# Causal mask of a self attention: TensorE's mask matmuls replaced by VectorE's add-and-maximum, head by head

## The reference, cut to what matters

```python
causal_bias = jnp.where(i[None, :] <= i[:, None], 0.0, NEG)[None, None]
for l in range(N_LAYERS):
    h = rmsnorm(x, n1[l])
    qkv = h @ Wqkv[l].T + bqkv[l]
    q, k, v = jnp.split(qkv, 3, axis=-1)
    q = apply_rope(split_heads(q, H), cos, sin)
    k = apply_rope(split_heads(k, H), cos, sin)
    s = jnp.einsum('bhqd,bhkd->bhqk', q, k) * scale + causal_bias
    o = merge_heads(softmax(s) @ split_heads(v, H)) @ Wo[l].T + bo[l]
    x = x + o
    # ... cross attention with 77 keys, then a gated feed forward
```

## Time and profile before

| | |
|---|---|
| median of three runs | 2097.03 us (2095.99 to 2102.07) |
| the profiled execution's own time | 2108.02 us |
| its span | 2106.3 us |
| mean granted TensorE clock | 0.936 of full speed |
| busy: TensorE / VectorE / ScalarE / GpSimd | 86% / 67% / 51% / 37% |
| self attention of layers 0, 1, 2, 3 begins (first reduction of maxima) | 657, 1029, 1366, 1699 us |

### The profile page before, as it was taken

The page is one execution under the profiler, slowest core; times in us unless marked ns, Lnnn a source line. Parts: engine busy times, 40 slices in busy tenths (PEclk is TensorE's granted clock), DMA queues, the critical chain, the costliest instruction groups (busy, mean ns, idle before and its releaser), DMA issues. The chain is left out here.

```text
span 2106.3 us, 34605 instructions
## 1 busy us (share of the span) xinstructions
PE 1821.6 (86%) x12966; PEld 1123.3 (53%) x12971; DVE 1414.7 (67%) x3427; ACT 1067.3 (51%) x1523; POOL 785.3 (37%) x1131
## 2 busy tenths in 40 slices
PE   5978998584787898899899899999989999989978
PEld 4556665363454444565544464644555554456557
DVE  8667676552776877875577874577786466787475
ACT  2655655121453465564466566366656446656510
POOL 4423334403613554431455341255443154533130
PEclk9999998587787899999999999999999999999989
DMA  7443343121000000132000033000014000004200
GB/s 226 112 135 101 103 108 94 52 77 43 23 1 13 1 1 13 32 101 56 16 1 1 1 95 81 28 1 2 1 53 117 7 16 2 1 24 101 52 1 21
DMA packets 69995, 100.91 MB, mean 48 GB/s; under 512 B 17126, under 2 KB 35438, under 8 KB 69188
## 3 DMA queue, kind: packets, MB, share of 16 engines
q1 hardware_dynamic: 60612, 90.01, 14.9%
q0 software_dynamic: 9216, 8.69, 1.6%
HBM read 52.43 MB, written 12.38 MB: 31 GB/s over the span
## 5 line engine op out<-in xcount | busy, mean ns | idle before, releaser
L1778 DVE TENSOR_REDUCE maxima<-wide 128x2 f32<-128x512 f32 (+3 forms) x512 | 405.9, 818 | 133.7 <-PE wide L831 130.3
L2014 ACT ACTIVATE prob<-wide 128x768 f32<-128x768 f32 (+1 forms) x384 | 332.1, 881 | 146.0 <-PE wide L831 145.9
L1937 ACT ACTIVATE prob<-wide 77x1024 f32<-77x1024 f32 x256 | 257.8, 1017 | 91.9 <-PE wide L831 87.5
L831 PE MATMUL wide<-q_g 32*128 32x256 f32 (+3 forms) x2048 | 266.1, 390 | 38.2 <-ACT prob L2014 18.1
L2256 POOL TENSOR_SCALAR_AFFINE_SELECT prob<-prob 128x256 f32<-128x256 f32 (+1 forms) x384 | 184.8, 487 | 292.6 <-ACT prob L2014 291.0
L1454 DVE TENSOR_REDUCE maxima<-wide 128x8 f32<-128x616 f32 x256 | 202.8, 795 | 115.0 <-PE wide L831 109.4
L831 PEld LDWEIGHTS wide<-q_g 32*128 32x128 f32 x2048 | 138.4, 186 | 203.7 <-issue 99.8
L2078 POOL TENSOR_TENSOR rstd<-moments,cst 128x4 f32<-128x4 f32 x88 | 90.4, 1027 | 364.2 <-DVE moments L1342 171.5
L1858 ACT ACTIVATE q_g<-wide 128x1024 fp32r<-128x1024 f32 x128 | 131.1, 1024 | 185.0 <-PE wide L831 185.0
L831 PE MATMUL wide<-kx,q_g 128*128 128x312 f32 x512 | 180.7, 418 | 8.3 <-DVE maxima L1454 5.8
L2163 POOL DMA_DIRECT2D masked_k<-kx x224 | 121.3, 546 | 178.2 <-PE wide L831 177.0
(11 more groups left out here) (249 smaller groups left out, 3087.2 us busy)
## 6 DMA issues: line engine op xcount, KB each, us to landing
masked_q<-q_g SPq DMA_DIRECT2D x448, 64.0 KB
masked_q<-mask_l SPq DMA_DIRECT2D x84, 308.0 KB
masked_k<-kx POOLq DMA_DIRECT2D x224, 19.5 KB, 1.9
A<-in_w SPq DMA_DIRECT2D x2, 2048.0 KB, 11.9
unit_w<-in_unit_w SPq DMA_DIRECT2D x8, 448.0 KB, 3.8
ffn_w<-in_ffn_w SPq DMA_DIRECT2D x4, 768.0 KB, 4.7
slots_in<-v_third SPq DMA_DIRECT2D x1, 2560.0 KB, 12.4
prob<-slots_in SPq DMA_DIRECT2D x8, 320.0 KB, 3.3
```

The lines of the kernel that those rows point to most:

```text
L831: return e.matmul(out, lhsT, rhs, start=start, stop=stop, is_transpose=turn)
L1778: e.tensor_reduce(top[:, t, h], v[:, :, at0:at0 + P * t + P], AX.X, ALU.max, negate=True).then_inc(*made("max", *([("free", tile)] if t == ...
L1937: e.activation(p[0:SC, :], s[0:SC, :], ACT.Exp, bias=0.0, scale=1.0).then_inc(*made("exp", pb, ("free", tile)))
L2014: e.activation(pv, sv, ACT.Exp, bias=0.0, scale=8 ** -0.5).then_inc(*made("exp", pb, ("free", tile)))
```

## The change

TensorE's mask matmuls are gone, and with them the bf16 mask `causal_b` and its cast at the start. The constant "causal" is twice as wide: 512 bf16 numbers packed in 256 words, zeros for 384 keys and then the triangle, so that its last n columns are the mask of a block of n keys. VectorE reads the scores of one head and one block from PSUM, adds that mask, writes the sum back to the same place in PSUM and gives the maximum of the row: `tensor_tensor_reduce`, 16 in a group in place of 8. It has no negation, so that the maxima are stored as they are and the rows of the keys hold -1 in place of 1.

```diff
-for _n, _w in (("ident", P), ("causal", P), ("cumul", P), ("cos", NI * 8), ("sin", NI * 8),
+for _n, _w in (("ident", P), ("causal", S // 2), ("cumul", P), ("cos", NI * 8), ("sin", NI * 8),
...
+        causal = const("causal").bitcast(BF)
...
-                        mm(s[:, at1:at1 + P * t + P], qk[r, 0, P * t:P * t + P], qk[r, 1, 0:P * t + P],
-                           start=t == blocks[0], stop=False)
+                        i_mm = mm(s[:, at1:at1 + P * t + P], qk[r, 0, P * t:P * t + P], qk[r, 1, 0:P * t + P],
+                                  start=t == blocks[0], stop=t == blocks[-1])
                     at0 += P * t + P
-
-                for c in range(2):
-                    bank = s[:, S * c:S * c + S].rearrange("p (i k) -> p i k", i=NI)
-                    i_mm = mm(bank[:, blocks[0]:blocks[0] + len(blocks), :], ident_b[:, :],
-                              causal_b[:, :].unsqueeze(1).broadcast_to([P, len(blocks), P]), start=False)
                 i_mm.then_inc(*made("scores", tile))
...
-            e.tensor_copy(causal_b[:, :], const("causal")).then_inc(*made("begin"))
...
                 for t in blocks:
-                    e.tensor_reduce(top[:, t, h], v[:, :, at0:at0 + P * t + P], AX.X, ALU.max, negate=True).then_inc(
-                        *made("max", *([("free", tile)] if t == blocks[-1] else [])))
-                    at0 += P * t + P
+                    n = P * t + P
+                    for c, i in enumerate(heads_in):
+                        part = s[:, S * c + at0:S * c + at0 + n]
+                        e.tensor_tensor_reduce(part, part, causal[:, S - n:S], 1.0, NEG, ALU.add, ALU.max,
+                                               top[:, t, i:i + 1]).then_inc(
+                            *made("max", *([("free", tile)] if (t, c) == (blocks[-1], 1) else [])))
+                    at0 += n
...
-                e.memset(k_tok[:, :, :, MROW:MROW + 2], 1.0).then_inc(*made("clear"))
+                e.memset(k_tok[:, :, :, MROW:MROW + 2], -1.0).then_inc(*made("clear"))
...
-    put("causal", np.where(r[None, :] > r[:, None], NEG, 0.0))
+    late = np.concatenate([np.zeros((P, S - P)), np.where(r[None, :] > r[:, None], NEG, 0.0)], 1).astype(np.float32)
+    put("causal", (late.view(np.uint32) >> 16).astype(np.uint16).view(np.float32))
```

More of the change, by code:

```diff
@@ L156 @@
     tensor_reduce = tensor_copy = memset = reciprocal = bn_stats = bn_aggr = affine_select = dma_start = anything
-    indirect_dma_start = anything
+    indirect_dma_start = tensor_tensor_reduce = anything
 def interleaved(items):
@@ L532, in build @@
         ident_b = sb("ident_b", [P, P], BF)
-        causal_b = sb("causal_b", [P, P], BF)
         cumul_b = sb("cumul_b", [P, 2 * P], BF)
@@ L1772, in causal_max @@
                 heads_in, blocks = CAUSAL_TILES[k]
-                h, at0 = slice(heads_in[0], heads_in[-1] + 1), 0
-                v = s[:, :].rearrange("p (i k) -> p i k", i=2)
+                at0 = 0
                 for w in need(tile):
```

## The result

The changed kernel takes 2147.39 us (median of four runs, 2144.1 to 2151.03). Four runs of the kernel before on the same chip have a median of 2099.55 (2095.99 to 2104.32). The ratio is 1.0227, 95% interval 1.0196 to 1.0258: 48 us slower. The forecast was slower, 2125 us with 2072 to 2235 as its range.

The account below looks back on a forecast made before the run. TensorE was taken to bound the steady groups before, changing places with VectorE after. Terms of +10, +9 and +10 us gave +29, rounded to +28: 2097 + 28 = 2125 us, range 2072 to 2235.

Parts of the forecast that it names:

- TensorE's saving: Six pairs of mask matmuls gone from each head group: about 1.4 us a group, 5.6 us a batch less TensorE time.
- The pair's fixed part: Fixed cost of each new two-instruction VectorE operation, 16 a group: taken as 0.16 us, between 0.14 and 0.31.
- The lower end: Lowest cost thought possible for a new VectorE pair, both instructions overlapping with neighbours: 0.07 + 0.07 = 0.14 us.
- The built-in waits of the ring: VectorE waits in the ring of three tiles: 0.4 us before tile three, 0.66 before tile five, together 1.1 a group.
- The steady batch: Four successive head groups go from 45.74 to 46.5 us, 0.8 more; 12 such batches give +10 us.
- The first batch: First batch of layers 1 to 3: 2.0 us for the VectorE-filled group, about 1 for the rest; 3 x 3 = +9.
- Layer 0: Its first five groups, where VectorE is the bound already, pay 2.0 us each: +10 us.
- The clock: Side term: a mean TensorE clock of 0.9 adds some 4 us to its batch, which VectorE's 41 still cover.
- A: Rival: TensorE's time wins, a pair costs 0.14 us, the wait before tile three vanishes; faster, 2080 us; chance 0.24.
- B: Rival: VectorE's pairs don't overlap, 0.31 us each; much slower, 2265 us, or 2177 half way; chance 0.25.
- C: Rival: VectorE's new operation runs at half rate, a second step per element; +344 us, about 2470; chance 0.05.
- the terms of VectorE: Sum over 12 batches (+10), first batches of layers 1 to 3 (+9) and layer 0's first five groups (+10): +29 us.

Follow-up runs that it names:

- the filler: Changed kernel plus four zero-weight matmuls of 128 columns at each of 172 places behind which TensorE waits: 2122.24 us, ratio 1.0120 to the kernel before.
- e1_nomask: Kernel before with its mask matmuls taken out and nothing put in their place: 2091.66 us, ratio 0.9943 to the kernel before.
- e2_both: Changed kernel with the mask matmuls kept as well, so the mask is added twice: 2141.84 us, ratio 1.0199 to the kernel before.

## Why the prediction was right, and by what

The direction holds: slower, and 2147 is 22 us above the forecast, inside its range. The size holds partly by luck, since the parts didn't carry what I gave them.

- *TensorE's saving, 1.4 us a group.* Busy time fell by 1.08 (43.17 to 38.86 in a batch), and by itself that gives 1.8 us a batch of time. The part of the 5.6 that was on the path was a third, since masks also lay inside waits.
- *The pair's fixed part, 0.16 within 0.14 to 0.31.* It is 0.08 to 0.11: I had added 0.07 for the read, and it costs nothing inside a tile. The lower end wasn't one. Two starts with 512 elements lie 0.62 us apart, not 0.70. VectorE's busy time in a group rose by 1.14 on average (33.19 to 37.74 in a batch), not by 2.0, and its share is 82%, not 88%.
- *The built-in waits of the ring.* Right: 0.60 us before the third tile and 0.66 before the fifth in the group shown, where I had 0.4 and 0.66; by the table of shapes, the mean of all 64 groups is 0.46 before the third and fourth tile together and 0.55 before the fifth and sixth. With them neither engine is full: 38.9 and 37.7 of 46.1 us.
- *The steady batch, +0.8.* It is +0.37 in the second batch and less in the others at their fastest; the nine such batches of layers 1 to 3 gave +2 us.
- *The first batch, 3 us each.* It is 4.7, fastest against fastest. The first group alone went from 7.30 to 9.10, which looks like the 2.0 forecast and isn't: with the masks kept and the clock at 1.00 it took 8.36, so that VectorE gave 1.06 and the masks' going, with the clock at 0.74, the rest. Of what came after it, with the clock at 0.50 to 0.65, a part is that the kernel before is taken there at its best (9.29 us, where its other layers had 10.60 and 12.26).
- *Layer 0, +10.* It is +10.7, by luck. The forecast put 10 us on its first five groups, where VectorE is the bound; these went from 80.06 to 82.74 us, by 2.7. The other 8 us came in the ten groups behind them, with the clock at 0.86 in place of 0.94, and the filler took back 6.2.
- *The clock, nothing, since VectorE's time would cover it.* This is the step that failed. Some steady groups did go below 1.00, as I had said they would, but a slow group took 13.29 us in place of 11.99 and wasn't covered. The filler gave 25 us (22 by the ratios, 32 by parts), about half of the 48. VectorE covers TensorE only if it is the bound; here both wait for each other in turn, so a slower TensorE adds to the chain.
- *Rivals.* A is out: the trade by itself was never faster. The 0.14 of its pair was even undercut, yet the batch didn't fall. B and C are out by the rows above.

Layer 0's first five groups and the ten behind them, before and then after:

```profile
657.05:737.11 80.06, 64.18 (x420) 35.04 (x418) 64.90 (x157) 34.39 (x54) 33.10 (x44) 0.78 0.03 9
737.11:859.38 122.27, 111.68 (x980) 60.52 (x981) 88.62 (x154) 75.13 (x102) 56.20 (x87) 0.94 0.02 7
...
639.39:722.13 82.74, 60.52 (x360) 33.45 (x360) 70.74 (x278) 34.48 (x54) 33.05 (x44) 0.73 0.03 9
722.13:852.37 130.24, 108.86 (x859) 57.73 (x860) 100.48 (x395) 75.55 (x102) 56.02 (x86) 0.86 0.02 6
```

So +28 came out near +48 since the errors had opposite signs: the terms of VectorE came to 29 us where at most 14.2 + 2.2 + 4.5 = 21 were found (4.5 is layer 0 with the filler against before, and the 14.2 hold low clock too), and the clock's to nothing where 22 to 25 or more were. That the mask matmuls held the clock is shown by e1_nomask (clock loss 18.7 us where masks alone go, 3.6 in e2_both where they stay with the new operation) and by the filler, which gives time only where they are gone. Open is how the first batches and the long stretches divide between VectorE, the clock and chance, and the size in single places: a clock that falls in one group and not in its twin of another layer (11.99 and 13.29 us) can't be forecast from these rows.

## What to carry to other kernels

Taking work from the busiest engine pays only for the part that stood on the chain; the part inside waits gives nothing back, and on TensorE it can cost the clock. Before taking matmuls away, look at what idle times they leave and at the granted clock of the groups behind them; here four matmuls of zeros inside each of the longer waits brought most of it back, and the same ones where nothing waited cost time.

Where two engines take turns in a ring of three tiles, neither share of busy time names the bound: added time of the less busy engine was paid here at 0.40 to 0.45 of its size in a steady batch at full clock. And compare a group with its twins in the other layers before naming a cause: the same code took 9.29, 10.60 and 12.26 us in one execution.

## What was not expected of the hardware

- A fused add and maximum over PSUM, written in place, runs at 1.05 ns an element like a reduction, and the read of its accumulator (140 ns) is hidden when another main instruction follows without a wait: 0.08 to 0.11 us of fixed part a pair. Two heads in one reduction save little: 683 ns each against 1219 for both.
- TensorE's clock fell to the 1.2 GHz level behind idle times of 0.3 to 1.4 us with matmuls between them, after 5.45 us in which TensorE was busy 2.77; where it was busy 4.78 of 5.35 in the same place before, it stayed at 2.4 GHz. In the group behind that one it fell in two of three layers even before the change.
